# The ninth tap's third tile in the outlook stage: ScalarE copies its replicated weights out of PSUM and GpSimd multiplies them, where VectorE did both in one instruction

## What is computed

```
a = softmax((x @ W_attn + b_attn).reshape(B, H*W, heads, 9))     # 6 heads, 3 x 3 taps
v = pad(x @ W_v + b_v)                                           # one pixel of border
y[p, h, :] = sum over K of a[p, h, K] * v[p shifted by tap K, h, :]
x = x + y @ W_proj + b_proj                                      # x normalized ahead of it
```

## Time and profile before

| what | value |
|---|---|
| runs | 3619.59, 3623.78 and 3627.0 us, median 3623.78 us |
| profiled execution: span of its instructions | 3620.7 us |
| busy shares of the span | PE 94%, DVE 77%, POOL 66%, ACT 53% |
| one chunk of the outlook stage, from one line 383 of TensorE to the next | 19.61 us |

### The profile page before, as it was taken

How to read it: one execution, slowest core, us unless ns; L and a number is a source line. 1 busy time by engine, 2 the same in 40 slices (tenths; PEclk the granted TensorE clock), 3 DMA queues, 4 the chain that set the end, 5 groups by cost and what they waited for, 6 DMA issues and landing times.

```text
span 3620.7 us, 108243 instructions
## 1 busy us (share of the span) xinstructions
PE 3391.4 (94%) x39908; PEld 1934.4 (53%) x39908; DVE 2774.4 (77%) x4977; ACT 1918.9 (53%) x4114; POOL 2401.7 (66%) x1888
## 2 busy tenths in 40 slices
PE   6999999999999999999999999999999999999999
PEld 3456654566445664456643666346663466634666
DVE  4977779677796777977779677787777877788776
ACT  3445654456545564456643656446564366644565
POOL 2867747677486774767747677577765777567775
PEclk7999999999999999999999999999999999999999
DMA  4732227322372224712246222561215512165222
GB/s 106 139 88 65 78 71 141 74 75 68 88 138 59 82 68 89 145 53 77 78 93 128 67 71 69 106 130 56 80 58 118 117 56 83 59 130 107 61 74 63
DMA packets 204359, 317.64 MB, mean 88 GB/s; under 512 B 16922, under 2 KB 176154, under 8 KB 203802
## 3 DMA queue, kind: packets, MB, share of 16 engines
q0 software_dynamic: 31936, 148.66, 21.1%
q1 hardware_dynamic: 171866, 161.61, 15.2%
HBM read 45.97 MB, written 38.54 MB: 23 GB/s over the span
## 4 chain that ended last, share of the span: by engine, by line
PE 65%; issue 11%; ACT 8%; DVE 8%; POOL 4%; DMA 3%; ACTq 1%; DVEq 0%; SPq 0%; POOLq 0%
PE P L737 5%; PE P L754 5%; PE P L481 5%; PE P L338 5%; PE P L336 5%; PE P L345 4%; PE P L706 4%; PE P L344 4%; PE P L682 3%; DVE prod L1435 3%; DMA prod<-prod 3%; PE P L685 2%; PE P L339 2%; ACT kbd L1110 2%; PE P L772 2%
## 5 line engine op out<-in xcount | busy, mean ns | idle before, releaser
L1777 POOL TENSOR_TENSOR sp__70<-sp__70,mx 128x588 f32<-128x588 f32 x512 | 600.1, 1172 | 603.5 <-DVE mx L1550 602.2
L1435 DVE TENSOR_TENSOR prod<-P,vpad 128x896 f32<-128x896 f32 (+1 forms) x768 | 790.3, 1049 | 131.2 <-PE P L481 118.2
L1784 POOL TENSOR_TENSOR sp__70<-sp__70,rc 128x588 f32<-128x588 f32 x512 | 600.3, 1172 | 21.5 <-DVE rc L1560 21.5
L1540 DVE TENSOR_TENSOR sp__70<-P,relb 128x196 f32<-128x196 f32 x512 | 184.2, 360 | 466.6 <-PE P L706 466.5
L1137 ACT ACTIVATE pt<-P 98x294 f32<-98x294 f32 x1024 | 429.7, 421 | 176.6 <-PE P L737 175.7
L481 PE MATMUL P<-at,sel 108*128 108x448 bf16 x1512 | 428.0, 362 | 58.2 <-DVE prod L1435 32.9
L1697 POOL DMA_DIRECT2D prod<-prod x216 | 202.0, 938 | 376.7 <-DVE prod L1435 371.7
L737 PE MATMUL P<-ident,sp__70 113*98 113x113 f32 x3072 | 390.3, 263 | 17.3 <-ACT pt L1137 10.3
L1550 DVE TENSOR_REDUCE mx<-sp__70 128x12 f32<-128x588 f32 x512 | 389.5, 761 | 9.4
L1557 DVE TENSOR_REDUCE sm<-sp__70 128x12 f32<-128x588 f32 x512 | 386.9, 756 | 10.7 <-ACT sp__70 L1127 10.5
L737 PEld LDWEIGHTS P<-ident,sp__70 113*98 113x98 f32 x3072 | 325.7, 129 | 111.6 <-issue 51.3
(11 more groups left out here) (244 smaller groups left out, 7430.8 us busy)
## 6 DMA issues: line engine op xcount, KB each, us to landing
prod<-prod POOLq DMA_DIRECT2D x216, 672.0 KB, 5.5
vbd<-vs SPq DMA_DIRECT2D x512, 147.0 KB
xin<-in_x SPq DMA_DIRECT2D x126, 336.0 KB, 4.1
out<-ot SPq DMA_DIRECT2D x184, 168.0 KB, 2.3
out<-ot SPq DMA_DIRECT2D x80, 84.0 KB
wn<-in_L_conv_qkv_weight SPq DMA_DIRECT2D x2, 432.0 KB, 6.3
wno<-in_L_conv_proj_weight SPq DMA_DIRECT2D x2, 144.0 KB, 6.4
self<-in_sel SPq DMA_DIRECT2D x3, 91.1 KB
```

The costliest lines, as they stand in the source:

```text
L1435: tt(by_row(dst), by_row(P[:, b:b + len(op), 0:CT]), val, ALU.mult).then_inc(prod_ok, 1)
L1777: tt(per_head(sp_[:, b, :]), per_head(sp_[:, b, :]), spread(mx[:, b, :]), ALU.subtract).then_inc(t_sub, 1)
L1784: tt(per_head(sp_[:, b, :]), per_head(sp_[:, b, :]), spread(rc[:, b, :]), ALU.mult).then_inc(p_norm, 1)
```

## The change

In chunks 0 to 5 of each pair the multiplication of step 13 (448 pixels of tap 8, tile 2) is taken from VectorE. ScalarE copies the weights from bank 2 into a new buffer `rep8` (`keep_rep`, its last instruction of the chunk), and GpSimd multiplies that buffer with the values into slot 3 (`product8`, ahead of add 8 in the program of the next chunk). The semaphore `rep_kept` tells TensorE (step 1 of the next chunk, which writes bank 2) and GpSimd that the copy is done, `prod8_ok` tells that the product is. The last chunk is as before. `prod_ok` counts 13 products in chunks 0 to 5, and all its waits are rewritten for that.

```
+DVE_OPS = NOPS - 1
+PAIR_OPS = CHUNKS * DVE_OPS + 1
...
-                    pe.wait_ge(prod_ok, ONE + NOPS * G + n - 1)
+                    if n == 1 and c > 0:
+                        pe.wait_ge(rep_kept, ONE + LAST * i + c)
+                    elif n != 1:
+                        pe.wait_ge(prod_ok, ONE + PAIR_OPS * i + DVE_OPS * c + max(n - 1, 0))
...
+                def keep_rep(c):
+                    act.wait_ge(rep_mm, ONE + NOPS * (G0 + c + 1))
+                    act.wait_ge(prod8_ok, ONE + LAST * i + c)
+                    go(rep8[:], P[:, 2, 0:CT], ACT.Copy).then_inc(rep_kept, 1)
+
                 def outlook(c):
...
                         keep_weights(G + 1, c + 1, 1, V_BANK)
+                        keep_rep(c)
...
                     for n in range(NOPS):
-                        product(c, n)
+                        if c == LAST or n < DVE_OPS:
+                            product(c, n)
...
                     if k == KK - 1:
-                        pool.wait_ge(prod_ok, ONE + NOPS * G + LAST_OP[k] + 1)
+                        pool.wait_ge(prod_ok, ONE + PAIR_OPS * i + DVE_OPS * (c + 1))
+                        pool.wait_ge(prod8_ok, ONE + LAST * i + c + 1)
...
+                def product8(c):
+                    G = G0 + c
+                    pool.wait_ge(rep_kept, ONE + LAST * i + c + 1)
+                    pool.wait_ge(merged[1], 16 * (G + 1))
+                    pool.wait_ge(v_kept, ONE + T * (G + 2))
+                    by_row = lambda ap: ap.rearrange("p (r n) -> p r n", n=W)
+                    tt(by_row(prod[:, SLOT_OF[8], 2, :]), by_row(rep8[:]),
+                       vpad[:, 2, c * ROWS + 2:(c + 1) * ROWS + 2, 2:2 + W], ALU.mult).then_inc(prod8_ok, 1)
+
                 def outlook(c):
                     if c > 0:
+                        product8(c - 1)
                         add(c - 1, 1, 8)
                         add(c - 1, 2, 4)
```

More of the change, by code:

```diff
@@ L149, in mixer @@
         s_base, u_base, z_base = base, base + S_BYTES, base + S_BYTES + U_BYTES
-        xn, lg, smx, ssh, ssum, srec, comb, at = plan(
+        xn, lg, smx, ssh, ssum, srec, comb, at, rep8 = plan(
             s_base, ("xn", [128, T, CT], F32), ("lg", [128, CT], F32), ("smx", [TT, SOFT // KK], F32),
             ("ssh", [TT, SOFT], F32), ("ssum", [TT, SOFT // KK], F32),
-            ("srec", [TT, SOFT // KK], F32), ("comb", [TT, NT * T, SPLITS, QK], F32), ("at", [QK * SPLITS, 2 * T * CT], BF16))
+            ("srec", [TT, SOFT // KK], F32), ("comb", [TT, NT * T, SPLITS, QK], F32), ("at", [QK * SPLITS, 2 * T * CT], BF16),
+            ("rep8", [128, CT], F32))
         vbd0, xw = plan(s_base, ("vbd0", [2 * N, NW, 2, C], F32), ("xw", [128, 2, T, RT], F32))
@@ L186, in mixer @@
         sp_low = sem("sp_low"); a_turned = sem("a_turned"); a_kept = sem("a_kept")
-        rep_mm = sem("rep_mm"); prod_ok = sem("prod_ok"); tail_ok = sem("tail_ok"); padd_ok = sem("padd_ok")
+        rep_mm = sem("rep_mm"); rep_kept = sem("rep_kept"); prod8_ok = sem("prod8_ok"); prod_ok = sem("prod_ok"); tail_ok = sem("tail_ok"); padd_ok = sem("padd_ok")
         merged = [sem(f"merged{n}") for n in range(MERGES)]
@@ L200, in mixer @@
                    g_ready, xn_ok, l_mm, l_kept, l_turned, v_mm, v_kept, border_ok, s_max, s_sub, s_exp, s_sum,
-                   s_rec, s_norm, s_back, sp_rest, sp_low, a_turned, a_kept, rep_mm, prod_ok, tail_ok,
+                   s_rec, s_norm, s_back, sp_rest, sp_low, a_turned, a_kept, rep_mm, rep_kept, prod8_ok, prod_ok, tail_ok,
                    padd_ok, o_mm, x1_kept, x1_stat, x1_wrap, xw_first, xw_ok, xr_ok, vs_zero, q_mm, q_kept,
@@ L1467, in finish_last @@
                     two, one = P[:, 0:2, 0:CT], P[:, 2, 0:CT]
-                    dve.wait_ge(prod_ok, ONE + NOPS * (G + 1) - 1)
+                    dve.wait_ge(prod_ok, ONE + PAIR_OPS * (i + 1) - 1)
                     tt(two, two, seven[:, 0:2, :], ALU.add).then_inc(tail_ok, 1)
-                    dve.wait_ge(prod_ok, ONE + NOPS * (G + 1))
+                    dve.wait_ge(prod_ok, ONE + PAIR_OPS * (i + 1))
                     tt(one, one, seven[:, 2, :], ALU.add).then_inc(tail_ok, 1)
@@ L1694, in merge @@
                     G = G0 + c
-                    pool.wait_ge(prod_ok, ONE + NOPS * G + LAST_OP[2 * n + 1] + 1)
+                    pool.wait_ge(prod_ok, ONE + PAIR_OPS * i + DVE_OPS * c + LAST_OP[2 * n + 1] + 1)
                     pool.sem_inc(stage_due, 1)
@@ L1738, in _ @@
                 tt(psum_p[:], psum_p[:], slot(4), ALU.add).then_inc(padd_ok, PADD - 1)
-                pool.wait_ge(prod_ok, ONE + NOPS * (G0 + CHUNKS))
+                pool.wait_ge(prod_ok, ONE + PAIR_OPS * (i + 1))
                 pool.sem_inc(stage_due, 1)
```

## The result

The changed kernel takes 3688.1 us (median of four runs, 3683.8 to 3695.6), the kernel before 3624.4 us on the same chip (four runs): a ratio of 1.0179, with a 95% interval of 1.0164 to 1.0193, so 64 us slower. Forecast were 49 us more, and 3650 to 3695 us.

The account below looks back on a forecast made before the run. GpSimd's ring of dependent work, 19.42 us a turn, was taken as full, within about 1% of TensorE and VectorE. 48 x 1.09 = 52.3 us, less 3, gave +49 on 3623.8: 3673 us, range 3650 to 3695 us.

Parts of the forecast that it names:

- GpSimd's ring: GpSimd's turn in the outlook stage, add 8 through merges 0, 1, 3 to the next add 8: 19.42 us, without slack.
- VectorE's relief at nothing: VectorE loses one 611 ns product per chunk, 29 us in all; counted as no gain because VectorE waits for TensorE.
- ScalarE's copy at nothing: ScalarE's added copy of 448 columns, about 634 ns, counted as free: 0.33 us in hand before TensorE's step 1.
- The price of 1.09 us: GpSimd's new multiplication ahead of add 8: 1.01 us by rate plus 0.08 gap, between 0.97 and 1.55, 48 times.
- the sum of 49: Total growth forecast in us: 48 x 1.09 = 52.3, less 3.
- The 3 us taken off: Deduction at the stage end for two pairs whose last merge waited for a product (1.56 us in the third pair).
- The ring as a fixed sum: Each turn's pieces, including 5.82 us from merge 1 to add(c, 0, 2), stay; everything moves by 1.09 us per turn.
- The turn of 20.4 to 20.9 us: Sign of being right: one GpSimd turn, add 8 to add 8, takes this long in the profile after.
- the rival with 3651 to 3662 us: Partly absorbed: stage end follows TensorE (about 3662 us), with merge 1's landing also shorter 3651 us; chance 0.10.
- L494 waits for GpSimd's y from the third chunk on: TensorE's L494 has 1.71 us in hand, used up by the second turn, then stands about a microsecond per chunk.
- the same lateness seen from elsewhere: Products of steps 0, 4, 6 and 9 wait for additions that free their slots; counted as no further cost.
- The window stages as before: Sign of being right: the windows stage, where nothing is changed, takes as long as before.

## Why the prediction came out as it did

The mechanism was right, one term of the sum was too small.

- **GpSimd's ring is full although GpSimd is 79% busy**: shown, by the same spare instruction at two places (+63 us in the ring, nothing in the gap). The Trainium skill ("Perfetto Trace Analysis", section Identifying the Most-Contended Engine), whose measure for GpSimd is the busy share, would have let the work go there; here the kernel with GpSimd's higher share, 68% with the spare instruction in the gap, is the fast one.
- **VectorE's relief at nothing**: right to 6 us of 29, by the kernel without the multiplication, and not told apart from nothing, since the spare multiplication in the gap ended 4 us lower too. (VectorE's 19.22 of 20 us is some 3% below TensorE's 19.89, not within 1% as the prediction writes.)
- **ScalarE's copy at nothing**: right. In the changed kernel it begins at 583.73 and takes 0.55 us, and TensorE's step 1 begins at 584.80: 0.5 us in hand where 0.33 were forecast. The timelines of ACT and PE:

```profile
583.73 0.55 ACT L1059 ACTIVATE rep<-P 128x448 f32<-128x448 f32 x1
```

```profile
584.80 0.55 PE L487 MATMUL P<-at,sel 108*128 108x448 bf16 x2
...
595.03 0.55 PE L487 MATMUL P<-at,sel 108*128 108x448 bf16 x2 [0.47 <-DVE prod L1447]
...
597.46 0.64 PE L500 MATMUL P<-y,wp_s 64*128 64x448 f32 x1
```

- **The price of 1.09 us**: the term that was too small, inside its bounds of 0.97 to 1.55. It was put together as "448/1344 of 3034 ns = 1.01 us" and "a gap more ... 0.08". Measured: a record of 1.05 and a gap of 0.22, 1.27 us from multiplication to add 8 where it follows a wait, and 1.56 less 0.30 elsewhere. The gap was read off two additions of which the second carries its wait for the first itself; in the changed kernel a semaphore and a register instruction stand between. 48 x 0.18 = 8.6 us of the 11 by which the outlook stages exceed the sum of 49. The Trainium skill ("GPSIMD Engine Reference", section 4.1, Engine selection) was nearer with its factor of two: 1.27 against VectorE's 0.611 us is 2.1, while the record alone, 1.05, is 1.7.
- **The 3 us taken off** for two pairs whose last merge had waited: too much. Their stages grew by 7.1 us, those of the other six by 7.65 in the mean, so 1.2 us in all. That is the other 2 us of the 11.
- **The ring as a fixed sum**: right in total, by luck in part. The prediction took 5.82 us from one turn for the landing and start behind merge 1 and moved everything by the same price. In the mean over the pairs this piece took 6.28, 6.14, 5.82, 6.37 and 6.18 us in the five turns before, and 6.47, 6.04, 5.87, 5.85 and 6.47 after. So the fourth turn absorbed 0.5 us and the first and the last added to the price; over a pair the shifts cancel to 0.1 us. No run shows why they fall so.
- **The turn of 20.4 to 20.9 us**, from add 8 to add 8: 20.7 to 20.9 in the three middle turns, 21.0 to 21.6 in the first and the last, which the prediction did not have. Each of the stages grew by at least 6.9 us, so the rival with 3651 to 3662 us fell.
- **"L494 waits for GpSimd's y from the third chunk on"**: wrong. The add into y ends at 593.88 + 3.34 = 597.22 and L500 (the former L494) begins at 597.46 without a wait. In the first five of a pair's seven projections it waits for y in no pair, in the sixth in three of eight (0.16 to 1.11 us; before, in four). TensorE is held up earlier in the chunk, at step 8 by 0.47 us, by VectorE, which has waited for the additions that free its slots. In VectorE's timeline of the changed kernel these are step 0 and step 4:

```profile
585.17 1.09 DVE L1447 TENSOR_TENSOR prod<-P,vpad 128x896 f32<-128x896 f32 x1 [1.92 <-POOL psum_p L1727]
...
590.33 1.09 DVE L1447 TENSOR_TENSOR prod<-P,vpad 128x896 f32<-128x896 f32 x1 [0.55 <-POOL psum_p L1727]
```

  The prediction named this path too and took it for the same lateness seen from elsewhere. It is the one that acts; the sum doesn't change by it.
- **The window stages as before**: +6.0 us in these two profiles. In the profiles of the experiments the same seven stages, with nothing changed in them, took 2159.2 to 2167.5 us, so this lies within their spread; what makes it is not settled.

## What to carry to other kernels

An engine's idle time can be filled only where it idles: follow the work from one issue of a DMA over its landing to the next, and if that ring closes without slack, every instruction put into it costs its full length, whatever the busy share. Price a short instruction by the distance from its start to the next one's, with the waits that will stand between them, and put those that have long been met ahead of it. And before an order is changed to let a transfer start earlier, see what the DMA engines carry at that time: here two transfers side by side took half as long again as one.

## What the hardware showed besides

The gap between two dependent instructions on GpSimd was 0.08 us where the wait for the first was the first one of the second, 0.14 where a semaphore instruction stood between them, and 0.22 where a semaphore and a register instruction did. A multiplication of 448 columns took 1.05 us after a wait, 1.34 directly behind the issue of merge 3, and 1.65 behind that of merge 1.

Near the end of seven of the changed kernel's eight outlook stages the granted clock of TensorE falls to the lower of its two levels for some microseconds. Four windows of the kernel with the shorter add 8, before and in the tail of the first pair and then of the second, where it doesn't fall:

```profile
182.00:192.00 10.00, 8.36 (x43) 3.28 (x43) 7.87 (x10) 4.23 (x7) 6.25 (x5) 1.00 0.80 156
192.00:202.00 10.00, 9.78 (x31) 6.26 (x32) 7.79 (x13) 0.00 (x0) 9.36 (x5) 0.52 0.65 126
...
629.20:639.20 10.00, 8.74 (x45) 3.40 (x43) 7.83 (x10) 4.77 (x8) 5.59 (x5) 1.00 0.76 148
639.20:649.20 10.00, 8.61 (x40) 4.43 (x40) 9.59 (x16) 0.00 (x0) 9.70 (x6) 1.00 0.62 121
```

At 0.52 of full speed (1.2 GHz for nearly the whole stretch) TensorE is busy 9.78 of 10 us with fewer matmuls; ahead of it it was busy 8.36 of 10 us, and 8.74 ahead of the stretch that kept 2.4 GHz. From the last multiplication to VectorE's y the first of these pairs took 23.9 us, the second 22.7; the other pairs of this kernel took 23.1 to 23.9 us with a fall (three) and 22.6 to 22.8 without (three). In the changed kernel, where GpSimd is later, this part takes 23.5 to 23.8 us in all pairs, also in the one without a fall (the sixth), so it shows as no part of the loss.
